# A two-layer graph attention kernel: the far maximum taken from rows not yet normalised, conversions of tables 0 to 2 on ScalarE, layer 1's first masks ordered anew

## The chip, the cores and the metric

One core of a Trainium2 chip runs the kernel. The metric is the device time of one execution in microseconds (us); the median of three runs of the kernel before is 506.02 us (504.74 to 507.35).

## What is computed

Two attention layers over one dense 0/1 matrix `adj` of 4096 x 4096, each followed by a residual and a layer norm. Cut to what matters:

```python
def attention(h, s, d, adj):              # N = 4096, D = 64
    e = leaky_relu(s[:, None] + d[None, :], 0.01)
    return softmax(where(adj > 0, e, -9e15), axis=1) @ h
x = layernorm(x + attention(x, x @ a[:64], x @ a[64:], adj))
wh = x @ weight_w
x = layernorm(x + attention(wh, wh @ a_src, wh @ a_dst, adj) + bias)
```

## The kernel before, in words

The exponential of a leaky ReLU of s + d is a product of a row factor and a column factor on either side of the sign of s + d. So each layer needs two 0/1 masks, `pos` and `neg` (edges with s + d above and below zero), and two weighted value tables, one for each sign. TensorE multiplies masks (fp8) by tables (bf16). A table entry in f32 is split into three bf16 parts hi, mid and lo, side by side in one row of 195 columns, so the product keeps f32 accuracy.

The 4096 output rows are cut into 8 supers (`NS`) of 512 rows, the 4096 columns into 4 granules (`NG`) of 8 tiles (`GT`). `granule(layer, s, g)` is 4 x 8 x 2 = 64 products of 128x195 into `acc` (L418). Here (l,s,g) stands for layer, super and granule. For each granule of layer 0 DMA loads 2 MB of `adj`, VectorE narrows it to bytes (`to_bytes`, L791), transposes it in blocks (`turn`, L803) into `kept` (granules 0 and 1, kept for layer 1) or `turned` (2 and 3, spilled to HBM and reloaded in layer 1). ScalarE writes the signs of s + d (`signs`, L557, eight 128x512 activations) into one of four slots of `neg`; a slot is free when the products of the granule four earlier are done. `mask` on VectorE turns sign and adjacency into `neg` and half of `pos` (L817, L820); GpSimd makes the other half of layer 0's `pos` (L979). In layer 1 VectorE makes the whole of `pos` (L823).

When a super's products are done, VectorE reads the accumulators (`read_acc`, L829), combines and divides (`average`, L847 to L856), adds the residual (`residual_sum`, L861) and takes the moments (`moments`, L866 to L870); GpSimd makes the inverse deviation (`inverse_std`, L968 and L972); ScalarE normalises (`normalize`, L570). TensorE turns the normalised rows (`turn_x1`, L431), ScalarE copies them (`copy_x1`, L577 and L579), TensorE projects them with the weights (`project`, L401) and ScalarE copies the result to `wh1` (`copy_wh`, L585), whose last column is the column score d.

Layer 1 wants, before its first product: the column scores of the tiles, their maximum for a shift (near half: supers 0 to 3; far half: supers 4 to 7), the exponentials `wts` (`exps`, L535 and L536), the tables (`split`, L725 to L730: product, cast to hi, subtract, cast to mid, subtract; all on VectorE, with one scratch `rest1` that lies in `narrow`), and a column mean (`mean1`, L351). The maximum goes through TensorE twice (`turn_max`, L334; `column_max` on VectorE, L745; `spread_max`, L338). Tables 0 and 1 are built with the near shift and multiplied by a power of two later (`rescale`, L773). `scores1` (L371) makes the row scores and `score_row` (L320) the row of s for the signs.

The order of the work is written out by hand for each engine, and each engine runs its list in order. A wait is issued in the engine's own list, so all that stands behind it on that engine waits too. `step` makes VectorE wait for its own last instruction. DMA issues go out from SP and ScalarE. Around the boundary, ScalarE's list before is: signs(0,7,3), copy_wh(5), normalize(6), near exps, signs(1,0,0), half of signs(1,0,1), copy_x1(6), the other half, copy_wh(6), normalize(7), copy_x1(7), copy_wh(7), far exps, signs(1,0,2), signs(1,0,3). TensorE's is: granules to (0,7,3), turn_x1(6), score_row(1,1), scores1 of supers 0 to 3, project(6), scores1 of supers 4 and 5, turn_x1(7), project(7), two steps of mean1, turn_max(1), spread_max(1), four steps of mean1, granule(1,0,0), the last of mean1 and scores1, granule(1,0,1) and on.

## Time and profile before

| what | value |
|---|---|
| median of 3 runs | 506.02 us |
| the profiled execution, its own time | 507.45 us |
| its span in the trace | 505.7 us |
| mean granted TensorE clock | 0.926 |
| PE matmul busy | 447.5 us (88%) |
| VectorE (DVE) busy | 402.2 us (80%) |
| ScalarE (ACT) busy | 397.8 us (79%) |
| GpSimd (POOL) busy | 90.4 us (18%) |

The span is cut in 40 slices, each digit the busy share in tenths; PEclk is the granted TensorE clock in tenths of full speed, DMA the busy share of the DMA engines:

```profile
PE   0799778879979899897979979999999999999991
DVE  3789989889799898989887889794849586675844
ACT  2695269877978879887890938899899999999931
PEclk9987979997979999897997958999999999999997
DMA  8999999999999999999973100202030202102000
```

A slice is 12.6 us. DMA is busy up to slice 21 (some 265 us), where the last of `adj` has come: that is layer 0. From slice 24 on PE is at 9: that is layer 1. Between them lies the stretch that the change works on, where no engine is busy all the time. Start times in the rows below count from the start of the span.

### The profile page before, as it was taken

To read this page: it belongs to the slowest core of one execution; us is meant where nothing else is said; L and a number is where in the kernel's file an instruction comes from. 1 tells how busy PE (TensorE), PEld (TensorE's weight loads), DVE (VectorE), ACT (ScalarE), POOL (GpSimd) and SP (SyncE) were. 2 spreads that over 40 slices of the span, in tenths; PEclk is the share of its full clock that TensorE was granted. 3 is DMA by queue.
4 is the path that set the end of the run, shared out by engine and by line. 5 is a ranking of instruction groups with operands and counts; after the bars stand their busy time and mean duration, and the time that the engine had idled before them with its cause. 6 is when DMAs were issued, how large, how long until landed. Compare 5 with 4: busy or idle time off the path is not lost.

```text
span 505.7 us, 11789 instructions
## 1 busy us (share of the span) xinstructions
PE 447.5 (88%) x4420; PEld 417.1 (82%) x4420; DVE 402.2 (80%) x712; ACT 397.8 (79%) x619; POOL 90.4 (18%) x68
## 2 busy tenths in 40 slices
PE   0799778879979899897979979999999999999991
PEld 0379768868979698797969968999999999999991
DVE  3789989889799898989887889794849586675844
ACT  2695269877978879887890938899899999999931
POOL 0012221514225151421423020010101010101010
PEclk9987979997979999897997958999999999999997
DMA  8999999999999999999973100202030202102000
GB/s 186 251 237 277 286 262 291 313 303 312 313 312 329 302 324 315 319 306 318 329 207 126 43 0 3 84 2 96 1 93 0 93 10 83 55 38 93 3 12 10
DMA packets 80294, 87.71 MB, mean 173 GB/s; under 512 B 7298, under 2 KB 76162, under 8 KB 80258
## 3 DMA queue, kind: packets, MB, share of 16 engines
q1 hardware_dynamic: 45602, 52.98, 36.9%
q10 hardware_dynamic: 34656, 34.21, 25.0%
q8 instruction: 27, 0.44, 0.4%
q14 instruction: 9, 0.07, 0.0%
HBM read 77.74 MB, written 9.44 MB: 172 GB/s over the span
## 4 chain that ended last, share of the span: by engine, by line
issue 49%; DVE 22%; DMA 18%; PE 5%; POOL 4%; SPq 1%; ACT 0%; POOLq 0%; ACTq 0%; DVEq 0%
DMA stage<-in_adj 16%; DVE narrow L791 4%; PE acc L418 4%; DVE turned L803 3%; POOL small L968 3%; DVE pos L817 2%; DMA xn<-in_x 2%; DVE num L854 1%; DVE num L861 1%; DVE red L847 1%; DVE kept L728 1%; DVE bn L866 1%; DVE num L851 1%; DVE kept L725 1%; DVE neg L820 1%
## 5 line engine op out<-in xcount | busy, mean ns | idle before, releaser
L557 ACT ACTIVATE neg<-srow,dcol 128x512 int8 (+1 forms) x512 | 352.9, 880 | 10.4 <-issue 8.0
L418 PE MATMUL acc<-xy_old,pos 128*128 128x195 bf16 x1024 | 198.9, 263 | 22.8 <-POOL pos L979 20.0
L418 PE MATMUL acc<-xy_old,neg 128*128 128x195 bf16 x1024 | 198.6, 263 | 0.0
L418 PE MATMUL acc<-stage,pos 128*128 128x195 bf16 x1024 | 178.2, 248 | 0.0
L418 PE MATMUL acc<-stage,neg 128*128 128x195 bf16 x1024 | 178.1, 248 | 0.0
L418 PEld LDWEIGHTS acc<-xy_old,pos 128*128 128x128 fp8e4 x1024 | 107.5, 105 | 31.7 <-issue 29.8
L418 PEld LDWEIGHTS acc<-xy_old,neg 128*128 128x128 fp8e4 x1024 | 106.8, 104 | 1.6
L418 PEld LDWEIGHTS acc<-stage,pos 128*128 128x128 fp8e4 x1024 | 100.8, 98 | 4.7 <-issue 4.5
L418 PEld LDWEIGHTS acc<-stage,neg 128*128 128x128 fp8e4 x1024 | 100.3, 98 | 0.3 <-issue 0.3
L791 DVE TENSOR_SCALAR narrow<-stage 128x4096 uint8<-128x4096 int32 x32 | 74.1, 2316 | 16.3 <-DMA stage<-in_adj 15.4
L968 POOL TENSOR_TENSOR small<-small,minus_half 128x4 f32<-128x4 f32 x16 | 36.6, 2288 | 210.7 <-DVE small L869 210.7
L820 DVE TENSOR_TENSOR neg<-neg,kept 128x1024 uint32<-128x1024 uint32 x32 | 39.1, 1223 | 31.5 <-ACT neg L557 30.9
L829 DVE TENSOR_REDUCE red<-acc 128x130 f32<-128x390 f32 x64 | 33.1, 553 | 21.3 <-PE acc L418 21.2
L979 POOL TENSOR_TENSOR pos<-kept,neg 128x512 uint32<-128x512 uint32 x16 | 22.3, 1392 | 142.5 <-DVE neg L820 142.5
L820 DVE TENSOR_TENSOR neg<-neg,turned 128x1024 uint32<-128x1024 uint32 x32 | 39.2, 1224 | 2.2 <-ACT neg L557 1.7
L979 POOL TENSOR_TENSOR pos<-turned,neg 128x512 uint32<-128x512 uint32 x16 | 22.3, 1393 | 54.6 <-DVE neg L820 53.8
L570 ACT ACTIVATE x1s<-num,small 128x64 f32<-128x64 f32 x32 | 11.5, 429 | 20.9 <-POOL small L972 20.7
L570 ACT ACTIVATE xn<-num,small 128x64 f32 (+1 forms) x32 | 11.5, 429 | 18.9 <-POOL small L972 18.9
L315 PE MATMUL acc<-idf,xn 128*64 128x128 f32 x32 | 7.2, 418 | 15.8 <-DMA xn<-in_x 15.8
L315 PEld LDWEIGHTS acc<-idf,xn 128*64 128x64 f32 x32 | 5.2, 170 | 18.4 <-issue 12.2
L823 DVE TENSOR_TENSOR pos<-turned,neg 128x1024 uint32<-128x1024 uint32 x16 | 19.6, 1224 | 0.6
L823 DVE TENSOR_TENSOR pos<-kept,neg 128x1024 uint32<-128x1024 uint32 x16 | 19.6, 1224 | 0.5
(117 smaller groups left out, 337.2 us busy)
## 6 DMA issues: line engine op xcount, KB each, us to landing
stage<-in_adj ACTq DMA_DIRECT2D x64, 512.0 KB, 9.2
stage<-in_adj SPq DMA_DIRECT2D x64, 512.0 KB, 9.4
spill<-turned SPq DMA_DIRECT2D x16, 512.0 KB, 7.5
turned<-spill SPq DMA_DIRECT2D x16, 512.0 KB, 3.8
out<-x1s SPq DMA_DIRECT2D x8, 128.0 KB, 1.9
xn<-in_x SPq DMA_DIRECT2D x1, 768.0 KB, 17.0
kept<-in_x SPq DMA_DIRECT2D x4, 128.0 KB, 3.9
kept<-in_x ACTq DMA_DIRECT2D x4, 128.0 KB, 5.0
```

What stands on the lines that cost most here:

```text
L315: last = nc.tensor.transpose(acc[0:D, t % RB, b * P:(b + 1) * P], xn[:, t // 2 * (2 * RB) + t % 2 + 2 * b, :], idf[:, :])
L418: last = nc.tensor.matmul(acc[:, r, c * XW:(c + 1) * XW], masks[c][:, t // BYTES, t % BYTES, r * P:(r + 1) * P], xy[layer][:, g * GT + t, ...
L557: last = nc.scalar.activation(o[:, t // BYTES, t % BYTES, :], srow[:, bass.ds((s % 2) * 512, 512)], ACT.Sign, bias=dcol[:, layer, col:col ...
L570: last = nc.scalar.activation(to, y[:, r, :], ACT.Identity, bias=shift_n[:, r:r + 1], scale=rstd[:, r:r + 1])
L791: nc.vector.tensor_scalar(narrow[:, 0:GN].rearrange("p (b g j) -> p g b j", b=GB, g=GR), stage[:, g % SLOTS, :].rearrange("p (g b j) -> p ...
L803: nc.vector.transpose(words(mask_at(s, g)), words(narrow[:, 0:GN])).then_inc(turned_ready, 1)
L817: nc.vector.scalar_tensor_tensor(words(pos[:, g, :])[:, half], c[:, half], CODES, a[:, half], ALU.bitwise_xor, ALU.bitwise_and).then_inc(p ...
L820: nc.vector.tensor_tensor(c, c, a, ALU.bitwise_and).then_inc(neg_ready, 1)
L823: nc.vector.tensor_tensor(words(pos[:, g, :]), a, c, ALU.bitwise_xor).then_inc(pos_ready, 1)
L829: nc.vector.tensor_reduce(red[:, r, :, :].rearrange("p c f -> p (c f)").rearrange("p (c f) -> p c f", c=2), acc[:, r, 0:2 * XW].rearrange( ...
L968: nc.gpsimd.tensor_tensor(rstd, var, minus_half[:, :], ALU.pow).then_inc(std_ready, 1)
L979: nc.gpsimd.tensor_tensor(pos[:, g, :].bitcast(U32)[:, half], mask_at(s, g).bitcast(U32)[:, half], neg[:, g, :].bitcast(U32)[:, half], ALU ...
```

## The change

The far maximum is no longer taken from `wh1` of all four far supers. For supers 6 and 7 the score d is also worked out on VectorE from the rows y ahead of the norm: d = (y . v - mean(y) sum(v)) rstd, with v the projected weight (`vector_row`, `dot_rows`, `quick_columns`, `far_max`). ScalarE makes the hi and mid parts of tables 0 to 2 (`cast_part`), VectorE the product and the two subtractions (`table_start`, `table_rest`). The near maximum is taken one super earlier. In the last super of layer 0 (`last_body0`) the masks of super 7 stand ahead of average, residual and moments of super 6. Layer 1's masks are made in two parts (`negative`, `positive`) among the tables. TensorE's `turn_max(1)` and `spread_max(1)` move ahead of `turn_x1(7)`. GpSimd's last two `inverse_std` of layer 0 stand behind all its masks. The diff, cut:

```diff
+        v_row = sb("v_row", [P, D], F32)
+        v_sum = sb("v_sum", [P, 1], F32)
+        v_rep = x1s[:, :, :].rearrange("p r d -> p (r d)")[0:D, 0:P]
+        dots = sb("dots", [P, 2, RB], F32)
+        d_far = sb("d_far", [P, 2 * GT], F32)
...
-                    sp.wait_ge(pos_ready, (NS + s - 1) * NG + g + 1)
+                    sp.wait_ge(pos_made, (s - 1) * NG + g + 1)
...
+            def vector_row():
+                pe.wait_ge(w_ready, 4)
+                nc.tensor.matmul(misc[:, 128:128 + D], v_rep, idf[0:D, 0:D], start=True, stop=True)\
+                  .then_inc(row_psum, 1)
...
+                pe.wait_ge(row_ready, 1)
...
-                pe.wait_ge(pos_ready, k + 1)
+                pe.wait_ge([pos_ready, pos_made][layer], s * NG + g + 1)
...
                     last = nc.tensor.transpose(flip[0:D, b * P:(b + 1) * P], xn[:, rows, :], idf[:, :])
                 last.then_inc(x1_turned, 1)
-            def body0(s, first=False, last=False):
+            def body0(s, first=False, near=False, last=False):
+                if last:
+                    spread_max(0)
                 granule(0, s, NG - 1)
+                if last:
+                    pe.wait_ge(shift_ready, 3)
                 if not first:
                     turn_x1(s - 1)
                 if last:
...
                 else:
                     project(s - 1)
                 granule(0, s + 1, 1)
-                if last:
+                if first:
+                    vector_row()
+                if near:
                     pe.wait_ge(xT_ready, NS + s)
                     turn_max(0)
-                    spread_max(0)
                 granule(0, s + 1, 2)
             tables0()
...
             granule(0, 0, 1)
             granule(0, 0, 2)
             body0(0, first=True)
-            for s in range(1, NS - 2):
+            for s in range(1, NS - 3):
                 body0(s)
+            body0(NS - 3, near=True)
             body0(NS - 2, last=True)
             granule(0, NS - 1, NG - 1)
-            pe.wait_ge(shift_ready, 3)
             turn_x1(NS - 2)
             score_row(1, 1)
             pe.wait_ge(wh_kept, NS - 1)
...
             project(NS - 2)
             pe.wait_ge(wh_kept, NS)
             scores1(NS // 2, NS - 2)
+            turn_max(1)
+            spread_max(1)
             turn_x1(NS - 1)
+            pe.wait_ge(shift_ready, 4)
             project(NS - 1)
             pe.wait_ge(xT_ready, 2 * NS)
-            mean1(0, 2)
-            turn_max(1)
-            spread_max(1)
-            mean1(2, NS - 2)
+            mean1(0, NS - 2)
             granule(1, 0, 0)
+            pe.wait_ge(wh_kept, NS + 1)
             mean1(NS - 2, NS)
             scores1(NS - 2, NS)
             for g in range(1, NG):
...
+            def cast_part(g, part):
+                act.wait_ge(table_part, 2 * g + part + 1)
+                nc.scalar.copy(xy[1][:, g * GT:(g + 1) * GT, :, part, :].rearrange("p t c f -> p c t f"), rest1)\
+                  .then_inc(part_cast, 1)
...
-                        act.wait_ge(dcol_ready, 1 + g // (NG // 2))
+                        act.wait_ge(dcol_ready, max(g, 1))
...
                 if g + SLOTS < NG:
                     load_next(NS - 1, g)
             copy_wh(NS - 3)
-            normalize(0, NS - 2)
             act.wait_ge(shift_ready, 3)
             exps(1, slice(0, NEAR), minus_shift[:, 0, 0:1], minus_shift[:, 0, 1:2], exp_ready)
-            signs(1, 0, 0)
-            signs(1, 0, 1, range(0, GT // 2))
+            for g in range(2):
+                signs(1, 0, g)
+            for part in range(2):
+                cast_part(0, part)
+            normalize(0, NS - 2)
+            signs(1, 0, 2)
             copy_x1(NS - 2)
-            signs(1, 0, 1, range(GT // 2, GT))
+            cast_part(1, 0)
             copy_wh(NS - 2)
+            cast_part(1, 1)
             normalize(0, NS - 1)
+            act.wait_ge(shift_ready, 4)
+            exps(1, slice(NEAR, NEAR + GT), minus_shift[:, 1, 0:1], minus_shift[:, 1, 1:2], far_exp)
             copy_x1(NS - 1)
+            cast_part(2, 0)
             copy_wh(NS - 1)
-            act.wait_ge(shift_ready, 4)
-            exps(1, slice(NEAR, TILES), minus_shift[:, 1, 0:1], minus_shift[:, 1, 1:2], far_exp)
-            for g in range(2, NG):
-                signs(1, 0, g)
+            cast_part(2, 1)
+            act.wait_ge(dcol_ready, 3)
+            exps(1, slice(NEAR + GT, TILES), minus_shift[:, 1, 0:1], minus_shift[:, 1, 1:2], far_exp)
+            signs(1, 0, 3)
             signs(1, 1, 0)
             row_factors(1)
             with act.Fori(0, NS - 2) as s:
...
+                nc.vector.tensor_copy(v_rep, misc[0:D, 65:66].broadcast_to((D, P))).then_inc(w_ready, 1)
...
+            def vector_row():
+                dve.wait_ge(row_psum, 1)
+                nc.vector.tensor_copy(v_row[:, :], misc[:, 128:128 + D])
+                nc.vector.tensor_reduce(v_sum[:, :], misc[:, 128:128 + D], AX, ALU.add).then_inc(row_ready, 1)
...
-            def far_columns(n):
-                t = [slice(0, NEAR), slice(NEAR, TILES)][n]
-                dve.wait_ge(wh_kept, 1 + [NEAR_SUPS, NS][n])
+            def near_columns():
+                t = slice(0, NEAR)
+                dve.wait_ge(wh_kept, 1 + NEAR_SUPS)
...
-                dve.wait_ge(dcol_ready, n + 1)
+                dve.wait_ge(dcol_ready, 1)
...
+            def far_columns(g):
+                t = slice(g * GT, (g + 1) * GT)
+                dve.wait_ge(wh_kept, 1 + 2 * (g + 1))
+                if g == NG - 2:
+                    nc.vector.tensor_copy(d_far[:, 0:GT], wh1[:, t, D])
+                nc.vector.tensor_copy(dcol[:, 1, t], wh1[:, t, D]).then_inc(dcol_ready, 1)
+                dve.wait_ge(dcol_ready, g)
+                step(nc.vector.memset(wh1[:, t, D:E], 1.0))
+            def dot_rows(s):
+                k = s - (NS - 2)
+                step(V.tensor_tensor(x1s[:, :, :], y, v_row[:, :].unsqueeze(1).broadcast_to((P, RB, D)), ALU.mult))
+                step(V.tensor_reduce(dots[:, k, :], x1s[:, :, :], AX, ALU.add))
+                step(V.tensor_scalar(total, mv[:, :, 0], v_sum[:, :], None, ALU.mult))
+                step(V.tensor_tensor(dots[:, k, :], dots[:, k, :], total, ALU.subtract))
+            def quick_columns(s):
+                k = s - (NS - 2)
+                dve.wait_ge(std_ready, 2 * s + 1)
+                V.tensor_tensor(d_far[:, GT + k * RB:GT + (k + 1) * RB], dots[:, k, :], rstd, ALU.mult).then_inc(quick, 1)
+            def far_max():
+                dve.wait_ge(quick, 2)
+                nc.vector.tensor_reduce(mcol[:, 4:5], d_far[:, :], AX, ALU.max).then_inc(max_step, 1)
...
-            def near_tables(g):
-                step(split(1, g, rest1))
+            def table_start(g):
+                t = slice(g * GT, (g + 1) * GT)
+                shape = (P, 2, GT, E)
+                if g == NG - 2:
+                    dve.wait_ge(far_exp, 2)
+                V.tensor_tensor(rest1, wh1[:, t, :].unsqueeze(1).broadcast_to(shape),
+                                wts[:, :, t].unsqueeze(3).broadcast_to(shape), ALU.mult).then_inc(table_part, 1)
+            def table_rest(g, part):
+                t = slice(g * GT, (g + 1) * GT)
+                taken, lo = (xy[1][:, t, :, k, :].rearrange("p t c f -> p c t f") for k in (part, PARTS - 1))
+                dve.wait_ge(table_part, 2 * g + part + 1)
+                dve.wait_ge(part_cast, 2 * g + part + 1)
+                if part == 0:
+                    V.tensor_tensor(rest1, rest1, taken, ALU.subtract).then_inc(table_part, 1)
+                else:
+                    last = V.tensor_tensor(lo, rest1, taken, ALU.subtract)
+                    if g < NG // 2:
+                        step(last)
+                    else:
+                        last.then_inc(tables_ready, 1)
...
+            def positive(s, g):
+                k = (NS + s) * NG + g
+                dve.wait_ge(neg_ready, k + 1)
+                nc.vector.tensor_tensor(words(pos[:, g, :]), words(mask_at(s, g)), words(neg[:, g, :]),
+                                        ALU.bitwise_xor).then_inc(pos_made, 1)
+            def mask(layer, s, g):
+                negative(layer, s, g)
...
-                    dve.wait_ge(neg_ready, k + 1)
-                    nc.vector.tensor_tensor(words(pos[:, g, :]), a, c, ALU.bitwise_xor).then_inc(pos_ready, 1)
+                    positive(s, g)
...
                         residual_sum(0, s)
                     if g:
                         mask(0, s + 1, g - 1)
-                    if g == 3 and s == NS - 2:
-                        far_columns(0)
+                    if g == 2 and s == NS - 3:
+                        near_columns()
                     turn(s + 1, g)
                     if g == 1:
                         read_acc(0, s)
                     if g == 2 and s == 0:
                         source_vectors()
-                    if g == 3 and s == NS - 2:
+                    if g == 3 and s == NS - 3:
                         column_max(0)
                     if g == 3:
                         moments(0, s)
+                    if g == 3 and s == 0:
+                        vector_row()
+            def last_body0(s):
+                for g in range(NG):
+                    to_bytes(s + 1, g)
+                    if g == 0:
+                        mask(0, s, NG - 1)
+                        near_shift()
+                    if 0 < g < NG - 1:
+                        mask(0, s + 1, g - 1)
+                    turn(s + 1, g)
+                    if g == 1:
+                        read_acc(0, s)
+                    if g >= NG - 2:
+                        mask(0, s + 1, g)
+                average(0, s)
+                residual_sum(0, s)
+                moments(0, s)
+                far_columns(2)
             dots0()
             column_max0()
...
             row_factors0()
             for n in range(2):
                 dve.wait_ge(s_x[n], 16)
-            for s in range(NS - 1):
+            for s in range(NS - 2):
                 body0(s)
-            near_shift()
-            mask(0, NS - 1, NG - 1)
+            last_body0(NS - 2)
             dve.wait_ge(exp_ready, 5)
-            near_tables(0)
+            table_start(0)
+            negative(1, 0, 0)
+            table_rest(0, 0)
+            positive(0, 0)
+            dot_rows(NS - 2)
+            table_rest(0, 1)
+            quick_columns(NS - 2)
             read_acc(0, NS - 1)
             average(0, NS - 1)
             residual_sum(0, NS - 1)
             moments(0, NS - 1)
-            near_tables(1)
-            mask(1, 0, 0)
-            mask(1, 0, 1)
-            far_columns(1)
+            dot_rows(NS - 1)
+            table_start(1)
+            quick_columns(NS - 1)
+            far_max()
+            negative(1, 0, 1)
             column_max(1)
+            table_rest(1, 0)
             far_shift()
+            positive(0, 1)
+            table_rest(1, 1)
             rescale(0)
+            table_start(2)
             rescale(1)
-            dve.wait_ge(far_exp, 2)
-            far_tables(2)
-            mask(1, 0, 2)
+            table_rest(2, 0)
+            negative(1, 0, 2)
+            table_rest(2, 1)
+            positive(0, 2)
+            far_columns(3)
+            dve.wait_ge(far_exp, 4)
             far_tables(3)
             mask(1, 0, 3)
             row_factors1()
...
-            with pool.Fori(0, NS - 1) as s:
+            with pool.Fori(0, NS - 2) as s:
...
+            for g in range(NG):
+                positive(NS - 1, g)
+            inverse_std(0, NS - 2)
...
```

## Rows read from the trace of the kernel before

**Rows 1.** Busy time by stretch: start and end, length, each engine; layer 1.
```profile
316.00:494.80 178.80, 178.80 (x1998) 173.03 (x1997) 122.25 (x260) 163.74 (x254) 15.99 (x14) 1.00 0.14 47
```
**Rows 2.** Timeline of ScalarE near the end: start us, length us, what.
```profile
461.34 21.92 ACT L557 ACTIVATE neg<-srow,dcol 128x512 int8 x32
483.25 1.43 ACT L570 ACTIVATE x1s<-num,small 128x64 f32<-128x64 f32 x4
```
**Rows 3.** Waits, stretch 256 to 308 us: us in total, times, longest.
```profile
PE acc L418 <- POOL pos L979: 3.1, 1, 3.1
```
**Rows 4.** Timeline of TensorE between the layers.
```profile
254.41 1.12 PE L320 MATMUL srow<-xT,arep 64*128 64x512 f32 x2
...
285.25 0.60 PE L431 MATMUL flip<-idf,xn 128*64 128x128 f32 x4
...
292.14 3.57 PE L371 MATMUL misc<-v_src,xT 64*128 64x1 f32 x16 [0.55 <-ACT wh L585]
296.52 1.03 PE L431 MATMUL flip<-idf,xn 128*64 128x128 f32 x4 [0.81 <-ACT xn L570]
298.87 1.94 PE L401 MATMUL misc<-wext,xTs 65*128 65x65 f32 x8 [1.32 <-ACT xTs L577]
...
302.41 0.42 PE L334 MATMUL misc<-idf,mcol 128*1 128x128 f32 x1
...
303.71 3.78 PE L351 MATMUL flip<-wh,onesN 128*128 128x256 f32 x8
307.29 0.37 PE L418 MATMUL acc<-stage,pos 128*128 128x195 bf16 x1
```
**Rows 5.** Timeline of VectorE.
```profile
240.87 0.56 DVE L866 BATCH_NORM_STATS2 bn<-num 128x6 f32<-128x64 f32 x4
...
242.16 2.29 DVE L791 TENSOR_SCALAR narrow<-stage 128x4096 uint8<-128x4096 int32 x1
...
273.51 0.28 DVE L745 TENSOR_REDUCE mcol<-flip 1x1 f32<-1x128 f32 x1 [2.11 <-PE flip L334]
...
284.67 1.98 DVE L829 TENSOR_REDUCE red<-acc 128x130 f32<-128x390 f32 x4
286.68 0.70 DVE L847 TENSOR_TENSOR red<-red,ab 128x520 f32<-128x520 f32 x1
...
291.51 1.24 DVE L725 TENSOR_TENSOR narrow<-wh,wts 128x1040 f32<-128x1040 f32 x1
292.78 0.70 DVE L727 CAST stage<-narrow 128x1040 bf16<-128x1040 f32 x1
...
302.87 0.28 DVE L745 TENSOR_REDUCE mcol<-misc 1x1 f32<-1x128 f32 x1 [0.89 <-PE misc L334]
```
**Rows 6.** Timeline of ScalarE.
```profile
248.13 3.54 ACT L557 ACTIVATE neg<-srow,dcol 128x512 int8<-128x512 f32 x5
...
265.68 0.43 ACT L585 COPY wh<-misc 128x260 f32<-128x260 f32 x1
...
291.71 0.38 ACT L585 COPY wh<-misc 128x260 f32<-128x260 f32 x1
294.94 1.44 ACT L570 ACTIVATE xn<-num,small 128x64 f32<-128x64 f32 x4 [2.85 <-POOL small L972]
297.67 1.05 ACT L577 COPY xTs<-flip 64x512 f32<-64x512 f32 x1 [1.30 <-PE flip L431]
```
**Rows 7.** Busy time by stretch; third number from the right is the granted clock.
```profile
233.00:240.00 7.00, 6.06 (x38) 5.55 (x38) 6.82 (x10) 6.70 (x11) 1.29 (x2) 0.51 1.10 322
285.00:291.00 6.00, 6.00 (x49) 5.30 (x48) 5.60 (x22) 6.00 (x10) 0.00 (x0) 1.00 0.00 0
291.00:308.00 17.00, 13.96 (x52) 11.23 (x52) 14.93 (x30) 7.16 (x15) 3.00 (x2) 0.50 0.00 1
```
**Rows 8.** Groups of instructions by line: busy us, mean ns of one.
```profile
L516 ACT COPY kept<-kept 128x2048 f32<-128x2048 f32 x1 | 1.9, 1899 | 2.6 <-DMA kept<-in_x 2.6
L851 DVE TENSOR_TENSOR num<-red 128x260 f32<-128x260 f32 x16 | 6.9, 428 | 0.5
```

More of the change, by code:

```diff
@@ L172, in gat_kernel @@
         far_exp = sem("far_exp")
+        row_psum = sem("row_psum")
+        row_ready = sem("row_ready")
+        quick = sem("quick")
+        table_part = sem("table_part")
+        part_cast = sem("part_cast")
         scores_psum = sem("scores_psum")
@@ L186, in gat_kernel @@
         pos_ready = sem("pos_ready")
+        pos_made = sem("pos_made")
         sp_turn = sem("sp_turn")
@@ L762, in far_shift @@
                 step(nc.vector.tensor_scalar(factor_bits, drop[:, :], 127.0, 2.0 ** 23, ALU.add, ALU.mult))
-                nc.vector.memset(wh1[:, NEAR:TILES, D:E], 1.0)
                 step(nc.vector.tensor_tensor(far_n, far_n, near_n, ALU.max))
@@ L803, in turn, with negative @@
                 nc.vector.transpose(words(mask_at(s, g)), words(narrow[:, 0:GN])).then_inc(turned_ready, 1)
-            def mask(layer, s, g):
+            def negative(layer, s, g):
                 k = (layer * NS + s) * NG + g
```

## The prediction

> **What bounds the kernel now.** I read the busy time by stretch first. From 316 to 494.8 us TensorE is busy all the time at clock 1.00, while ScalarE and VectorE are not [rows 1]. These are the 31 granules (1,0,1) to (1,7,3) and six score rows of 1.1 us [rows 4]: (178.8 - 6.6) / 31 = 5.55 us a granule. So from the first product of layer 1 at 307.29 us (call this moment G) [rows 4] TensorE has a fixed 198.4 us to the end of the span. ScalarE's signs have a reserve: their last ends at 483.25, two mask instructions of 1.24 bring that to 485.8, and the granule that wants it starts at 494.8 - 5.55 = 489.3 [rows 1, 2, 5]. The change touches nothing of that part. Its worth is the move of G.
>
> Next I read the timelines of the three engines from 240 to 308. Layer 0's last products end at 285.25 and G is 22.0 us later [rows 4]. The chain into G is: read_acc(7) at 284.67, moments done at 291.5, normalize(7) 294.94, turn_x1(7) 296.52, copy_x1 297.67, project(7) 298.87, mean1 with the maximum in it, G [rows 4 to 6]. TensorE's clock is 1.00 to 291 and 0.50, the 1.2 GHz level, from 291 to 308, after one-column products and gaps [rows 7].
>
> **Layer 0's end.** In super 7 the masks pass average (with residual 3.5 us) and the far columns, and a wait of 2.11 us for turn_max(0) at 273.51 goes [rows 5]. TensorE's wait of 3.1 us for granule (0,7,1) at half clock goes too [rows 3]. I get masks of (0,7,1) some 2 us earlier, and its 64 products take 5.55 instead of 8.0 us: layer 0's products end near 280.3 instead of 285.25. That gain of 5 us counts only if read_acc(7), which is VectorE's, starts earlier.
>
> **A wait that moves one super earlier.** column_max(0) now stands in body0(5) ahead of moments(5), and waits for turn_max(0) behind granule (0,6,1). Counting two granules back from 253.9 (the turns just ahead of 254.41 take 0.5) that granule ends at 242.8 [rows 4]. It ran mostly at half clock (0.51) [rows 7]. VectorE is there at 240.87 [rows 5]. Transpose and reduction add 0.5, so everything from moments(5) on is 2.45 us late: to_bytes(7,0) at 244.6 instead of 242.16 [rows 5]. Behind it on ScalarE stands load_next(7,0), which waits for that narrowing, then copy_wh(4), normalize(5) and signs(7,1) at 248.13, from where ScalarE runs without a gap to copy_wh(5) at 265.68 [rows 6]. So ScalarE's stream is 2.45 late. DMA has one load ahead and covers it. Bounds: 0 (had that granule run at full clock, it would end 1.5 us earlier and the wait be 0.9; 0 is the floor) to 2.45. I take 2.45, the row.
>
> **Up to read_acc(7).** ScalarE: copy_wh(5) at 268.1, near exps 0.7 later, then 16 signs of 21.92/32 = 0.685 [rows 2]: signs(1,0,1) end at 279.8. Only then comes cast_part(0,0). VectorE is there earlier: mask (0,7,3) at 270.2, 4.8 for average, residual and moments (286.68 to 291.51), 0.5 for far_columns(2), 1.27 for the product, 1.24 for negative(1,0,0): 278 [rows 5]. The cast isn't in the trace. A ScalarE copy of 2048 f32 takes 1.90 [rows 8]; a strided one of 512 takes 1.05 [rows 6]. The first scales to 1.0 (with a fixed part 1.07), the second to 2.1. I take 1.07, since table rows are runs of 65 as in the first. Then: cast 280.9; table_rest(0,0) 282.2; positive(1,0,0) 283.4; dot_rows(6) 284.8 (two steps of 0.45 like L851 [rows 8], two small of 0.2; bounds 1.0 to 1.6); table_rest(0,1) 286.05; quick_columns 0.2. read_acc(7) starts at 286.25, 1.6 later than before. The 5 us are lost here: table 0 costs VectorE less, but 2.5 of masks, 1.35 of dots and the wait for the cast stand in their place.
>
> The Trainium skill speaks against this move ("ScalarE: Activation LUTs", rules for kernel authors): simple elementwise work belongs on VectorE, and an activation costs about 0.3 us and 0.83 ns an element, an estimate of 1.16 us here. The row has VectorE's cast at 0.70 [rows 5]. By the page's price the sum would be 0.3 longer.
>
> **From read_acc(7) to the far maximum.** 2.0 and 4.83 as before [rows 5], so moments end at 293.1. Then dot_rows(7) 1.35 and table_start(1) 1.27: 295.7. On ScalarE cast_part(1,0) stands ahead of copy_wh(6), so copy_wh(6) starts at 296.9, and not at 291.71 [rows 6]. TensorE's own path gives the same: normalize(6) now stands behind cast_part(0,1), at 283.3; turn at 284.9; at half clock after 4.5 idle us the turn and score row take 3.1, 64 score products 7.1 (32 take 3.57 [rows 4]), project 1.8: 296.9. I take 297.0. Behind copy_wh(6) TensorE does scores1 of supers 4 and 5 (3.57, plus 0.43 to start), so turn_max(1) is at 301.0. That is the order written: the early far maximum waits for these score products. VectorE has reached column_max(1) at 297.5 and stands there. Its next instruction is table_rest(1,0), which the cast (1,1) needs, and normalize(7) is queued behind that cast on ScalarE.
>
> **From there to G.** turn_max(1) to the end of column_max 0.74 (302.41 to 303.15) [rows 4, 5]; table_rest(1,0) 1.25; cast 1.1: normalize(7) at 304.1, against 294.94 [rows 6]. Then the steps of before: 1.58 to turn_x1(7), 1.15 to copy_x1, 1.2 to project(7) at 308.05 [rows 4, 6]. From project(7) to G took 8.42, and the maximum in its middle (302.41 to 303.71) 1.30 of it [rows 4]; that has gone. 308.05 + 7.12 = **315.2**, which is 7.9 us behind 307.29. Table 0 is ready (rescale(0) at 307.7), and the masks are.
>
> **What is hidden.** vector_row and the copies of v are 0.2 to 0.3 us each in super 0, in the shadow of loads. `row_ready` is set a whole granule before project(0) wants it. GpSimd's pow for super 6 waits for masks that end at 271 and is wanted at 283. SP's spills and reloads wait for masks that come earlier or are wanted 15 us later. far_columns(3) releases the far exps at 315.5; signs(1,0,3) end at 321.3, the mask at 324, wanted at G + 20 = 335. So layer 1 stays TensorE's, and its end moves with G.
>
> **Sum.** Against the execution of 507.45 us: +7.9 = 515.3. That execution lies 1.4 above the median of 506.02, so the forecast is 506.0 + 7.9 = **513.9 us**.
>
> **Rivals.**
> 1. *The wait in body0(5) is hidden.* Speaks for it: its length hangs on TensorE's half clock in one granule. Then the stream is 2.45 earlier, though TensorE's half-clock chain to copy_wh(6) moves with normalize(6): 511.5.
> 2. *The casts are slow*, as the strided row: 1.05 more in each of three serial casts: 517.1.
> 3. *The clock holds.* The idle stretch ahead of turn_x1(6) is 4.5 us and the far longer work after it is sparse; before, full clock lasted to 291 only since dense products ran to 285 [rows 7]. If it held 2.4 GHz all the way: 1.8 off the score products, 0.4 and 0.9 off turn and project, 2.7 off mean1, 0.4 in the first granule, 1.5 off the wait in body0(5): 7.7 off, 506.2, no change.
> 4. *Faster.* ScalarE's casts and the small steps of VectorE overlap so well that read_acc(7) follows layer 0's products at 280.3. The point from which it decides: cast_part(0,1) done by 279. Then all is 6 us earlier, 507.9, and with the clock of rival 3 (6.2 without the wait) 501.7. Against it: 16 signs stand ahead of the casts, and they can't end before 277.4 [rows 2, 6].
> 5. *The early maximum does nothing.* This is part of the forecast: turn_max(1) is 1.4 us earlier than 302.41 at most.
>
> **Chances.** Forecast 0.55, rival 1 0.16, rival 2 0.10, rival 3 or another cancelling 0.10, rival 4 0.09. About 0.5% (2.5 us) is what a measurement of this kernel can tell from no change. Slower 0.81, within 0.5% 0.11, faster 0.08. The range reaches from between rivals 3 and 1, 508.0, to a little over rival 2, 518.0.
>
> **What would show it.** Right: layer 0's products end near 280; read_acc(7) starts at 285 or later; ScalarE idles before cast_part(1,0) and copy_wh(6) starts after 294; VectorE waits over 2 us at column_max(1); normalize(7) after 301; first layer-1 product at 312 to 316, and no TensorE gap after it. Wrong: if G is at or before 307 with such a chain, if the clock is 1.00 between 290 and 308, or if TensorE shows waits for masks in layer 1, which would make G the wrong measure.

## The result and the profile after

The changed kernel takes 513.92 us (511.96 to 514.65, four runs), the kernel before 505.38 us in the runs beside it (504.41 to 507.35). The ratio is 1.0148, with a 95% interval of 1.0119 to 1.0176: slower by 7.5 us, 6.0 to 8.9 (the two medians lie 8.5 apart). The profiled execution took 514.64 us, its span is 512.6.

The page of the changed kernel, parts 1 and 2:

```profile
PE 447.8 (87%) x4422; PEld 418.9 (82%) x4422; DVE 403.6 (79%) x722; ACT 404.1 (79%) x627; POOL 90.5 (18%) x68
...
PE   0799688869979798898899759999999999999991
...
DVE  3789989889898898999998969475758595765854
ACT  2695269867898778898799736898989999999931
...
PEclk9987979998979899798999657999999999999997
```

ScalarE has 6.3 us more to do, six casts of 1.07 us. The difference isn't there, though: TensorE has the same work, and its slices 22 and 23 (from 0; 282 to 308 us) read 7 and 5 where the kernel before has 9 and 7, with a clock of 6 and 5 where it had 9 and 5. The boundary between the layers has grown.

The waits between 240 and 330 us (us in total, times, longest):

```profile
ACT stage L565 <- DVE narrow L862: 7.7, 3, 5.4
...
PE flip L449 <- ACT xn L599: 6.9, 2, 3.8
ACT stage L565 <- DVE narrow L852: 4.7, 2, 4.1
DVE mcol L816 <- PE misc L351: 3.9, 1, 3.9
```

The two of ScalarE are new, and the other two have grown: before, TensorE waited 0.81 us for the norm and VectorE 0.89 us for the transposed maximum [rows 4, 5]. ScalarE waits for VectorE's tables, VectorE for TensorE's transpose, TensorE for ScalarE's norm: three engines in a ring. The timelines show the ring once round. ScalarE (L565 `cast_part`, L614 copy_wh, L599 normalize, L606 copy_x1):

```profile
280.47 1.17 ACT L565 CAST stage<-narrow 128x1040 bf16<-128x1040 f32 x1
283.02 1.07 ACT L565 CAST stage<-narrow 128x1040 bf16<-128x1040 f32 x1 [1.38 <-DVE narrow L862]
...
296.24 1.07 ACT L565 CAST stage<-narrow 128x1040 bf16<-128x1040 f32 x1 [4.08 <-DVE narrow L852]
297.22 0.37 ACT L614 COPY wh<-misc 128x260 f32<-128x260 f32 x1
303.01 1.07 ACT L565 CAST stage<-narrow 128x1040 bf16<-128x1040 f32 x1 [5.42 <-DVE narrow L862]
303.98 1.43 ACT L599 ACTIVATE xn<-num,small 128x64 f32<-128x64 f32 x4
...
306.71 1.06 ACT L606 COPY xTs<-flip 64x512 f32<-64x512 f32 x1 [0.91 <-PE flip L449]
```

VectorE:

```profile
241.48 1.24 DVE L894 STREAM_TRANSPOSE turned<-narrow 128x1024 uint32<-128x1024 uint32 x1
243.64 0.28 DVE L816 TENSOR_REDUCE mcol<-flip 1x1 f32<-1x128 f32 x1 [0.92 <-PE flip L351]
243.85 0.58 DVE L965 BATCH_NORM_STATS2 bn<-num 128x6 f32<-128x64 f32 x4
...
252.22 2.29 DVE L882 TENSOR_SCALAR narrow<-stage 128x4096 uint8<-128x4096 int32 x1
...
259.32 2.29 DVE L882 TENSOR_SCALAR narrow<-stage 128x4096 uint8<-128x4096 int32 x1
...
286.77 1.97 DVE L928 TENSOR_REDUCE red<-acc 128x130 f32<-128x390 f32 x4
...
294.97 1.24 DVE L852 TENSOR_TENSOR narrow<-wh,wts 128x1040 f32<-128x1040 f32 x1
...
301.55 0.28 DVE L816 TENSOR_REDUCE mcol<-misc 1x1 f32<-1x128 f32 x1 [3.93 <-PE misc L351]
301.76 1.22 DVE L862 TENSOR_TENSOR narrow<-narrow,stage 128x1040 f32<-128x1040 f32 x1
```

TensorE:

```profile
301.14 0.37 PE L351 MATMUL misc<-idf,mcol 128*1 128x128 f32 x1
...
314.59 0.25 PE L436 MATMUL acc<-stage,pos 128*128 128x195 bf16 x1
```

Read ScalarE's lines from the third on. Cast (1,0) waits 4.08 us for table_start(1), and copy_wh(6) behind it starts at 297.22, where it was 291.71 [rows 6]. The score products and turn_max(1) follow, at 301.14. VectorE has stood for 3.93 us at column_max(1); only then can it subtract (301.76), ScalarE cast (303.01) and normalise (303.98, before 294.94 [rows 6]). The first product of layer 1 (G) is at 314.59, before 307.29 [rows 4].

I cut every profile at the same three moments: read_acc(7), G and the end of the span. All start times are those of VectorE's and TensorE's timelines.

| kernel | read_acc(7) | read_acc(7) to G | G to end | span |
|---|---|---|---|---|
| before | 284.67 | 22.6 | 198.4 | 505.7 |
| changed | 286.77 | 27.8 | 198.0 | 512.6 |

So 6.9 us of the span are 2.1 ahead of read_acc(7), 5.2 between it and G, and -0.4 behind G. The medians are 8.5 apart and these spans 6.9, since the profiled execution of the kernel before (507.45 us) was 2.1 above the median beside it, and that of the changed kernel 0.7.

### The profile page after: what moved, and what is told of

It reads as the page before. It is cut to its first block, busy times and chain, and to the rows that moved or that the text cites. A ratio compares the mean times of both kernels' runs of the same rounds, so it can differ in the third digit from the quotient of the medians.

```text
span 512.6 us, 11829 instructions
## 1 busy us (share of the span) xinstructions
PE 447.8 (87%) x4422; PEld 418.9 (82%) x4422; DVE 403.6 (79%) x722; ACT 404.1 (79%) x627; POOL 90.5 (18%) x68
## 4 chain that ended last, share of the span: by engine, by line
issue 48%; DVE 20%; DMA 16%; PE 6%; POOL 5%; ACT 3%; SPq 1%; POOLq 0%; ACTq 0%; DVEq 0%
DMA stage<-in_adj 14%; PE acc L436 5%; DVE narrow L882 4%; POOL small L1100 4%; DVE turned L894 3%; ACT neg L586 2%; DVE pos L908 2%; DMA xn<-in_x 2%; DVE num L960 1%; DVE num L953 1%; DVE red L946 1%; DVE neg L911 1%; POOL pos L1111 1%; DVE kept L770 1%; DVE kept L767 1%
## 5 line engine op out<-in xcount | busy, mean ns | idle before, releaser
L436 PE MATMUL acc<-xy_old,pos 128*128 128x195 bf16 x1024 | 195.0, 260 | 20.6 <-POOL pos L1111 17.7
L436 PE MATMUL acc<-xy_old,neg 128*128 128x195 bf16 x1024 | 194.7, 260 | 0.0
L436 PEld LDWEIGHTS acc<-xy_old,pos 128*128 128x128 fp8e4 x1024 | 106.2, 104 | 28.8 <-issue 27.3
L436 PEld LDWEIGHTS acc<-xy_old,neg 128*128 128x128 fp8e4 x1024 | 105.5, 103 | 1.3
L1100 POOL TENSOR_TENSOR small<-small,minus_half 128x4 f32<-128x4 f32 x16 | 35.2, 2200 | 218.6 <-DVE small L968 218.6
L928 DVE TENSOR_REDUCE red<-acc 128x130 f32<-128x390 f32 x64 | 33.3, 553 | 22.4 <-PE acc L436 22.4
L1111 POOL TENSOR_TENSOR pos<-turned,neg 128x512 uint32<-128x512 uint32 x16 | 24.7, 1542 | 55.5 <-DVE neg L911 54.9
L599 ACT ACTIVATE x1s<-num,small 128x64 f32<-128x64 f32 x32 | 11.5, 429 | 22.4 <-POOL small L1104 22.3
L894 DVE STREAM_TRANSPOSE turned<-narrow 128x1024 uint32<-128x1024 uint32 x16 | 19.8, 1239 | 0.2
```

The source lines that it names most:

```text
L436: last = nc.tensor.matmul(acc[:, r, c * XW:(c + 1) * XW], masks[c][:, t // BYTES, t % BYTES, r * P:(r + 1) * P], xy[layer][:, g * GT + t, ...
L599: last = nc.scalar.activation(to, y[:, r, :], ACT.Identity, bias=shift_n[:, r:r + 1], scale=rstd[:, r:r + 1])
L894: nc.vector.transpose(words(mask_at(s, g)), words(narrow[:, 0:GN])).then_inc(turned_ready, 1)
L928: nc.vector.tensor_reduce(red[:, r, :, :].rearrange("p c f -> p (c f)").rearrange("p (c f) -> p c f", c=2), acc[:, r, 0:2 * XW].rearrange( ...
L1100: nc.gpsimd.tensor_tensor(rstd, var, minus_half[:, :], ALU.pow).then_inc(std_ready, 1)
L1111: nc.gpsimd.tensor_tensor(pos[:, g, :].bitcast(U32)[:, half], mask_at(s, g).bitcast(U32)[:, half], neg[:, g, :].bitcast(U32)[:, half], ALU ...
```

## The experiments

### Is it the order of the boundary? e1, e2, e3

e1, on ScalarE:

```diff
             copy_x1(NS - 2)
-            cast_part(1, 0)
             copy_wh(NS - 2)
+            cast_part(1, 0)
```

> Changed kernel with one swap on ScalarE: copy_wh(6) ahead of cast_part(1,0). Yardstick: time from the start of read_acc(7) on VectorE to the first product of layer 1 (G); 27.8 us in the changed kernel (286.77 to 314.59), 22.6 in the one before. Theory (serial loop): copy_wh(6) no longer waits for table_start(1) but only for project(6), which ends at 295.6 at half clock, so it starts 1.5 us earlier and all behind it too: yardstick 26.3, time 1.5 us less than the changed kernel's 513.9. Rival (the casts on ScalarE and the extra VectorE steps cost by their own length, the order does not matter): 27.8 and 513.9.

Measured: 511.92 us, ratio to the kernel before 1.0115 (1.0061 to 1.0168). read_acc(7) to G 26.9, G to the end 198.0. copy_wh(6) waited for project(6) instead of the cast:

```profile
295.66 0.38 ACT L614 COPY wh<-misc 128x260 f32<-128x260 f32 x1 [5.08 <-PE misc L419]
```

That is 0.9 us off the yardstick and not 1.5, since its read_acc(7) was itself 1.6 us earlier (285.19) while project(6) kept its time: the granted clock from 284 to 291 was 0.50 here and 0.72 in the changed kernel's profile. 0.9 is little against what two profiles of the same order differ by (e7 below leaves the order alone and has 27.45), so it is the row that carries this reading.

e2, on TensorE:

```diff
-            scores1(NS // 2, NS - 2)
             turn_max(1)
             spread_max(1)
...
             mean1(NS - 2, NS)
+            scores1(NS // 2, NS - 2)
             scores1(NS - 2, NS)
```

> Changed kernel with turn_max(1) and spread_max(1) directly behind copy_wh(6), and the score products of supers 4 and 5 moved behind granule(1,0,0), where they take 1.8 us at full clock. Theory (serial loop): turn_max at 297.7 instead of 301.1, so column_max, table_rest(1,0), cast (1,1), normalize(7) and G are 3.45 us earlier: yardstick read_acc(7) to G 24.4 us; the 1.8 us come back behind G: time 1.6 less than 513.9, 512.3. Rival (order does not matter): yardstick 27.8, time 1.8 more, 515.7.

Measured: 514.44 us, ratio 1.0164 (1.0098 to 1.0230). read_acc(7) to G 24.6, as the theory had it. But G to the end was 201.6 and not 198.0 + 1.8: the moved products cost 3.6 us behind G, more than the 3.2 that they freed ahead of it. That is a miss of mine, taken up below.

e3, on ScalarE:

```diff
-            cast_part(1, 1)
             normalize(0, NS - 1)
+            cast_part(1, 1)
```

> Changed kernel with normalize(7) ahead of cast_part(1,1) on ScalarE. Theory (serial loop): normalize(7) at 297.6 instead of 304.0, but turn_x1(7) still stands behind spread_max(1) and copy_x1(7) behind the cast and the exponentials, which are released by the far shift: copy_x1(7) at 304.4 instead of 306.7, G 2.3 us earlier: yardstick 25.5, time 511.6. Rival (normalize(7) is late because its moments are late, not because of the cast): 27.8 and 513.9.

Measured: 511.25 us, ratio 1.0097 (1.0066 to 1.0127). read_acc(7) to G 25.25, G to the end 198.0. The ring is broken at its last link, and 2.6 us of the segment come back. Nothing was made cheaper in any of the three: the rival, that the added work costs by its length, has no room for these gains. They are read from the segments; by their times alone, e1 and e3 can't be told from the changed kernel, whose interval (1.0119 to 1.0176) theirs overlap.

### All three, and TensorE's clock: e4

> The three reorderings of e1, e2 and e3 together; every operation of the changed kernel is still there. Theory (serial loop): copy_wh(6) 295.7, turn_max(1) 296.6, column_max 297.6, normalize(7) 297.3, copy_x1(7) 300.7 instead of 306.7: G 6 us earlier, yardstick 21.8 us, 1.8 us come back behind G: time 509.7. So the order of the boundary is worth 4.2 of the 8.5 us; the rest lies ahead of read_acc(7) and in the score products. Rival (the added work itself, casts with their hand-overs, dots and masks, is the cost): at most 1 us less than the changed kernel, 513 or more.

Measured: 511.84 us, ratio 1.0121 (1.0065 to 1.0176). read_acc(7) to G 22.5, the 22.6 of the kernel before. All that the change added is in it; but the 32 score products of supers 4 and 5, 3.5 us between the two marks in the changed kernel (297.64 to 301.14), now stand behind G. So e4 by itself doesn't show that the ring was the whole 5.2 us; e5 below leaves these products in place. G to the end was 201.4, 3.4 more and not 1.8, and took most of the gain back. The same kernel a second time:

> e4 once more, in the same call as e10, to compare its time with e8's: segments of e4 repeat within 0.3 us (read_acc(7) to G 22.5, G to the end 201.4), time about 510.5 to 511.8. Rival (e4's segments were one execution's accident): G to the end at 200 or less.

Measured: 511.38 us, ratio 1.0079 (1.0049 to 1.0110); 22.4 and 201.3. The segments repeat.

What the 3.4 us are: the 64 score products in one piece, each one column wide, ran from 313.88 to 317.75. Behind them TensorE's records show

```profile
317.75 0.34 PE L436 MATMUL acc<-stage,pos 128*128 128x195 bf16 x1
```

and the granted clock of e4 in that stretch (third number from the right) is

```profile
312.00:322.00 10.00, 10.00 (x83) 9.39 (x81) 7.75 (x13) 9.43 (x15) 0.00 (x0) 0.83 0.22 75
```

The engine was busy all the time and its clock fell to the 1.2 GHz level (0.50 from 317.5 to 320.5): 2.0 us for the products themselves, and some 1.3 for the wide products behind them at half clock. The Trainium skill ("TensorE: Matmul & The Clock Gate", HAM oscillation) speaks of idle gaps; here there was none, only products of one column. e2 has the 64 in one piece too (317.86 to 321.59), and a clock of 0.56 from 321.3 to 324.5.

### With the clock kept: e8

e8 has e4's moves, the 32 products of supers 4 and 5 apart from the other 32, and column_max(0) late (e7):

```diff
             for g in range(1, NG):
                 granule(1, 0, g)
+                if g == 1:
+                    scores1(NS // 2, NS - 2)
```

> All work of the change kept, five moves undone or mended: copy_wh(6) ahead of cast_part(1,0), normalize(7) ahead of cast_part(1,1), turn_max(1) and spread_max(1) directly behind copy_wh(6), column_max(0) late as in e7, and the score products of supers 4 and 5 behind granule(1,0,1) and so apart from the 32 of supers 6 and 7. In e4 the 64 one-column products in one piece took 3.9 us, and TensorE's granted clock was 0.50 behind them (317.5 to 320.5), which made the next products 1.3 us longer. Theory: apart they leave the clock at 1.00, so G to the end is 199.9 us instead of 201.4; read_acc(7) to G 22.5; turn(6,3) to read_acc(7) 44.2. Time about that of the kernel before, plus 0.5: 506.5. Rival (the clock falls again, or row factors come too late behind the moved products): 508 or more.

Measured: 508.93 us, ratio 1.0054 (1.0029 to 1.0079). read_acc(7) 284.03, then 22.8, then 200.0. The clock held:

```profile
312.00:322.00 10.00, 10.00 (x101) 9.44 (x99) 5.33 (x5) 8.54 (x13) 0.00 (x0) 1.00 0.17 54
```

So of the 3.4 us behind G 1.4 came from the clock. The segments came out as expected; the time is 2.4 us above the 506.5 that I expected, as high as the rival had it, though neither of the rival's reasons is there: the clock held and TensorE has no wait from 307 to 340. Why it is that high stays open. It is still slower than the kernel before: mended, the work of the change buys nothing.

### The casts: e5

`cast_part` goes from ScalarE; on VectorE:

```diff
-                dve.wait_ge(part_cast, 2 * g + part + 1)
+                step(nc.vector.tensor_copy(taken, rest1))
```

> Changed kernel with the casts of tables 0 to 2 back on VectorE (0.70 us each) and no cast on ScalarE; all else stays in its order. Theory (the serial loop through ScalarE's queue is what delays G): copy_wh(6) and normalize(6), normalize(7) are free of the casts; turn_max(1) waits for the far maximum alone at 297.4, copy_x1(7) for the far shift at 302.2 instead of 306.7: read_acc(7) 0.7 us later, G at 310.1 instead of 314.6, read_acc(7) to G 22.6 us instead of 27.8, time 509.4 against 513.9. Rival (VectorE is the bound, so six casts of 0.7 us put back there cost 4 us): yardstick 28 or more, 515 or more.

Measured: 509.64 us, ratio 1.0047 (1.0020 to 1.0075). read_acc(7) 287.34, to G 22.0, to the end 198.2. On ScalarE the two operations that the casts had held are free of them:

```profile
291.09 0.38 ACT L614 COPY wh<-misc 128x260 f32<-128x260 f32 x1 [2.52 <-PE misc L419]
296.96 1.43 ACT L599 ACTIVATE xn<-num,small 128x64 f32<-128x64 f32 x4 [5.49 <-POOL small L1098]
```

Six casts more on VectorE, and G comes 5 us earlier, with the score products where they were. VectorE isn't the bound there; ScalarE's queue was. e4 keeps the casts and mends the order, e5 keeps the order and takes the casts out of the queue, and both bring the segment back to what it was before.

### The layer-0 side: e7, e6, b1, e9, e10

e7:

```diff
-                    if g == 3 and s == NS - 3:
-                        column_max(0)
...
                     if g == 0:
+                        column_max(0)
                         mask(0, s, NG - 1)
```

> Changed kernel with column_max(0) moved from super 5's end behind to_bytes(7,0), where TensorE has long made its transpose. Yardstick: start of turn(6,3) on VectorE to start of moments(5), 2.4 us in the changed kernel (241.48 to 243.85), 1.2 in the kernel before, and turn(6,3) to read_acc(7), 45.3 and 45.0. Theory: the wait goes, 1.2 instead of 2.4, the whole stream to read_acc(7) comes 1.1 us earlier (44.2) and the time falls by 1.1, to 512.8, which may not show in so few runs. Rival (the wait is hidden behind loads): read_acc(7) stays at 45.3.

Measured: 513.16 us, ratio 1.0119 (1.0073 to 1.0165). turn(6,3) to moments(5) 1.17 us instead of 2.37, turn(6,3) to read_acc(7) 43.9 instead of 45.3. The segment moved as the theory says; the times can't tell.

e6 takes the boundary behind moments(6) back to the old one. On VectorE, cut:

```diff
             dve.wait_ge(exp_ready, 5)
-            table_start(0)
-            negative(1, 0, 0)
-            table_rest(0, 0)
...
+            step(split(1, 0, rest1))
             read_acc(0, NS - 1)
...
+            step(split(1, 1, rest1))
+            mask(1, 0, 0)
+            mask(1, 0, 1)
+            far_columns(3)
+            far_max()
             column_max(1)
             far_shift()
```

> Only the layer-0 side of the change: near maximum one super earlier, super 7's masks ahead of average and moments, near shift and near exponentials early; the boundary behind it as in the kernel before (tables and casts on VectorE, far maximum from wh1 of all far supers), except that signs(1,0,2) go ahead of copy_wh(6). No dots from rows not yet normalised. Theory (the gain of layer 0's end was real and was spent on the new serial work): table 0 starts right behind moments(6), read_acc(7) about 2.5 us earlier than in the changed kernel, G behind it by 22.6 as before: 2.5 us less than the kernel before, 503.5. Rival (the early maximum's wait costs what the masks gain): no change against before, 506.

Measured: 507.08 us, ratio 1.0002 (0.9976 to 1.0029): the rival. turn(6,3) to moments(5) was 3.78 here. How long the wait is hangs on when TensorE ends granule (0,6,1), which took 6.8 us in the changed kernel's profile and 8.2 here. In the eight profiles with column_max(0) in this place the two starts are 2.4 to 3.8 us apart, in the others 1.2.

> The kernel before once more, for a second profile. It tells how much of a difference between two profiles is the spread of layer 0 under its loads: turn(6,3) started at 239.7 us in the first, and at 239.5 to 242.1 in the profiles of the changed kernels. Theory: this start moves by 1 to 2 us from execution to execution whatever the kernel, while the segments behind it repeat within 0.4: turn(6,3) to read_acc(7) 45.0, read_acc(7) to G 22.6, G to the end 198.4. Rival (the change itself makes layer 0 slower up to there): 239.7 again or less.

Measured: 507.36 us. Neither side had it right. turn(6,3) started at 241.57 instead of 239.71, so this start does move whatever the kernel; but read_acc(7) was at 284.80, 43.2 behind it and not 45.0. Its loads show why:

```profile
244.01 2.29 DVE L791 TENSOR_SCALAR narrow<-stage 128x4096 uint8<-128x4096 int32 x1
249.73 2.29 DVE L791 TENSOR_SCALAR narrow<-stage 128x4096 uint8<-128x4096 int32 x1 [0.42 <-DMA stage<-in_adj]
...
257.96 2.29 DVE L791 TENSOR_SCALAR narrow<-stage 128x4096 uint8<-128x4096 int32 x1 [1.06 <-DMA stage<-in_adj]
```

VectorE is waiting for loads in super 7, and a late start is made up there. In the changed kernel it isn't: none of super 7's narrowings waits for DMA (252.22 and 259.32 above have no such mark), because VectorE comes later than the loads. Six profiles with its layer-0 part (changed, e1 to e4, e4 again) have turn(6,3) to read_acc(7) at 45.1 to 45.4, and read_acc(7) at 284.9 to 286.8, 285.8 in the mean, against 284.7 and 284.8. So about 1 of the 2.1 us in the table above belongs to the change, and the rest to one profile's draw.

e9 is e6 with column_max(0) late as in e7.

> e6 (the layer-0 side of the change alone) with column_max(0) late, as in e7. In e6 moments(5) started 3.8 us behind turn(6,3), in the kernel before 1.2. Theory (that wait ate what the early masks gained): turn(6,3) to read_acc(7) 42.5 us instead of 43.7 in e6 and 45.0 before, read_acc(7) to G 22.5, G to the end 198: 2.4 us less than the kernel before, 504. Rival (the loads of super 7, issued behind the narrowings, take the gain away): no change against before, 506.4.

Measured: 505.07 us against 507.06 beside it, ratio 0.9953 (0.9930 to 0.9976): **faster than both kernels**, by 0.5% against the one before. turn(6,3) to read_acc(7) 42.5, read_acc(7) to G 22.6, G to the end 198.1, as expected. The layer-0 side had been worth something; one wait had eaten it. Which of its parts gives the gain I didn't take apart. e8 has the same layer-0 side with the dots and the casts on top, and 44.0 us for this stretch: they cost some 1.5 us ahead of read_acc(7). Another such wait is left in its VectorE timeline, near_shift's (L807) for spread_max(0):

```profile
250.91 0.23 DVE L807 TENSOR_SCALAR halvings<-per_ln,flip 128x2 int32<-128x2 f32 x1 [2.55 <-PE flip L355]
```

e10 moves it:

```diff
                         mask(0, s, NG - 1)
-                        near_shift()
                     if 0 < g < NG - 1:
                         mask(0, s + 1, g - 1)
+                    if g == 1:
+                        near_shift()
```

> e9 with near_shift one granule later, behind mask(7,0). In e9 near_shift(0) still waited 2.55 us on VectorE (to 250.91) for spread_max(0), which stands behind granule (0,6,2) on TensorE. Theory: that wait goes; what takes its place is the load of granule (7,1), which ended a wait at 249.7 in the second profile of the kernel before; so to_bytes(7,1) starts 2 to 3 us earlier, read_acc(7) 1 to 2 us earlier than in e9 (284.07), with the segments behind it as in e9 (22.6 and 198.1): 503.5 against 505.1. Rival (ScalarE's stream and the loads set the masks of super 7, not VectorE): read_acc(7) at 284 again and 505.

Measured: 504.49 us against 507.13, ratio 0.9958 (0.9937 to 0.9979). read_acc(7) at 280.19 and the span 501.6 in its profile, 41.1 us behind turn(6,3) instead of 42.5. A load wait has come into its place, that of granule (7,2) and not of (7,1) as expected (L868 is `to_bytes` here):

```profile
255.79 2.29 DVE L868 TENSOR_SCALAR narrow<-stage 128x4096 uint8<-128x4096 int32 x1 [1.10 <-DMA stage<-in_adj]
```

The profile says faster than e9, the ratios say the same. I leave it at that: e9 and e10 are both faster than the kernel before, by some 2 us, and not told apart.

## Why the prediction was right, point by point

**The measure.** G to the end of the span was to stay at 198.4; it was 198.0 to 198.2 in the changed kernel, e1, e3, e5, e6, e7 and e9. Right, and it made every experiment readable. (198.8 in e10, where the granted clock was 0.71 in the first 3.2 us behind G.)

**Layer 0's end.** Last product forecast near 280.3, found at 281.5; before 285.2. The gain was lost ahead of read_acc(7), as forecast.

**The wait in body0(5).** The mechanism was right, the size not: 2.45 forecast, 1.2 measured (2.37 from turn(6,3) to moments(5), before 1.16 [rows 5] with its turn at 239.71). The granule ahead of it ran at a mean clock of 0.72 (234 to 240), where the one before had 0.51 [rows 7]; the term rested on one draw of that. I also took the term as additive to the start of the kernel before. b1 shows that the start isn't fixed, and that the kernel before has slack there that the changed one lacks. So read_acc(7) at 286.77 against the forecast 286.25 is right in part by luck: the stream started 1.8 us later than the sum assumed, and the wait was 1.2 shorter. The two small instructions that GpSimd held up (last section) weren't in the sum either; the cast hid them, since VectorE still waited 0.71 us for it at 281.75.

**The casts.** 1.07 forecast from a plain copy, 1.07 measured in five of six (1.17 once). Rival 2, the strided rate, is out. The estimate of 1.16 from the Trainium skill ("ScalarE: Activation LUTs", rules for kernel authors) is near as well; the sums differ by 0.3 us.

**The ring.** copy_wh(6) 297.0 forecast, 297.22 found; turn_max(1) 301.0 and 301.14; normalize(7) 304.1 and 303.98; project(7) 308.05 and 307.86. e1, e3 and e4 showed the links one by one. Two lesser things in it were off. TensorE's clock didn't fall at turn_x1(6) but some us later (0.50 from 287 on, 0.72 from 284 to 291), so project(6) was done at 295.8 and not 296.9, and the cast alone held copy_wh(6). And G was 0.6 us earlier than forecast: 0.2 stood at project(7) already, and 0.4 came in the six mean1 steps, behind which the clock was back at the first wide product (0.25 us and not 0.37). That they are now in one piece doesn't explain it: in e2 they are too, and that product took 0.37; in e6 they are split, and it took 0.25.

**The rivals.** The clock at 0.50 from 291 to 308 puts rival 3 out; the 16 signs ahead of the casts, which hold the first of them until 280.47, put rival 4 out. Rival 1 is out too: e7 takes the wait away, and the stretch to read_acc(7) falls from 45.3 to 43.9 us. turn_max(1) came 1.3 us earlier than before (301.14 and 302.41), the 1.4 at most of the fifth. What I did not see as a case at all is that the layer-0 side alone could be made faster than before: I had its 5 us down as lost to work, and part was lost to two waits.

**The sum.** 7.9 forecast, 6.9 in the profiled span, 7.5 by the ratio. That the median (513.92) falls on the forecast (513.9) is luck: four executions spread over 2.7 us, and the terms above are off by up to 1.8 both ways.

## What to carry to other kernels

When work moves to a second engine in hand-written order, follow each queue and ask what stands behind every new wait; if engine A waits for B, B for C and C for something behind A's wait, the order of the queues weighs more than the lengths of the operations: here one swap (e3) gave 2.6 us back in the segment, while VectorE had been spared 0.7 us a cast. A result that is ready early is worth nothing while its consumer's engine has other waits ahead of it. Put a wait no earlier than where its producer has finished anyway, and look for the load wait that it will displace.

## What the runs showed of the hardware

A fully busy TensorE can lose its clock: 64 products of one column in one piece brought 0.50 behind them (317.5 to 320.5 in e4; 0.51 in its second run; 0.56 over a similar stretch of e2), 32 and 32 apart kept 1.00 (e8). In e4 that and the products together cost 3.4 us.

Two small VectorE instructions took 1 us longer than usual while GpSimd made a mask (VectorE, then GpSimd, in the changed kernel):

```profile
249.48 1.28 DVE L821 TENSOR_SCALAR halvings<-per_ln,flip 128x2 int32<-128x2 f32 x1 [0.18 <-PE flip L355]
...
273.19 1.39 DVE L950 TENSOR_TENSOR num<-red 128x260 f32<-128x260 f32 x1
```

```profile
249.48 1.26 POOL L1111 TENSOR_TENSOR pos<-turned,neg 128x512 uint32<-128x512 uint32 x1
...
272.72 1.57 POOL L1111 TENSOR_TENSOR pos<-turned,neg 128x512 uint32<-128x512 uint32 x1 [2.47 <-DVE neg L911]
```

The first takes 0.23 and the second 0.43 elsewhere, and here both end within 0.3 us of GpSimd's instruction. The other way round, GpSimd's instruction at 266.91 took 3.34 us instead of 1.27, behind the start of a narrowing of 2.29 at 266.82 on VectorE. In the profiles the first is 1.28 each time that near_shift starts together with GpSimd's mask (changed, e1 to e6), and 0.23 where it starts behind it (e7, e8, e9) or ahead of it (e10). That the two engines stood in each other's way is argued from these rows; no run was made for it. The second is 1.39 in every kernel with super 7's masks ahead of average. In e9 VectorE waits for no other engine from 251.2 until read_acc(7), so the 1 us is in its path there. Whether it can be had back wasn't tried.
